# Expert stage of a graph layer: two row fetches and two result scatters in flight, alternating semaphores, four result buffers

## The chip, the core and the metric

The kernel runs on one core of one Trainium2 chip. The metric is the device time of one execution in microseconds (us). Five engines take part: PE multiplies matrices (PEld is its loading of weights), DVE is the vector engine, ACT the scalar engine, POOL the engine that also issues the indirect DMAs, SP a sequencer that issues plain DMAs. Engines are kept in order with semaphores alone.

## The reference, cut to what matters

A graph convolution gives 12500 rows of 256 numbers; each row is then sent to the two best of 64 experts, a small two-layer network each, and their results are weighted and added:

```python
logits = x @ Wg + bg
vals, idx = jax.lax.top_k(logits, 2)
gates = jax.nn.softmax(vals, axis=-1)
# per expert e, at most 1024 rows (CAP):
h1 = gelu(buf[e] @ w1[e] + b1[e])      # 256 -> 512, float32
h2 = h1 @ w2[e] + b2[e]                # 512 -> 256, float32
core = zeros.at[tok].add(gate * h2)    # each row gets two results
```

After it come a batch norm, a residual and a layer norm over all rows.

## The kernel before

The kernel has three long stages, one after the other. The first sorts out the edges and the degrees. The second, `aggregate`, gathers edge rows, sums them on PE, and routes each row to its experts; it ends at about 2412 us. The third is `experts`, from about 2416 to 3455 us, and then `norms` closes the kernel. Only `experts` (line 1460) is touched.

In `experts` the work is cut into turns. A turn is 128 rows of one expert. An expert has from one to a few turns, and the 64 experts have 228 turns in all with these inputs. Four experts' weights are held at a time (`HELD`), 1152 KB each.

What a turn n needs, engine by engine:

- POOL fetches its 128 rows out of `x1_rows` in HBM into slot n % 4 of `ring`, by an indirect DMA (`fetch`, line 1565). The indices are in `rows_at`.
- ACT copies the slot to `xs` (`take`, line 1543). PE transposes `xs` (line 1674), DVE copies the result to `xst` (line 1621).
- PE multiplies with w1 in four pieces (line 1681), ACT applies the Gelu to each piece (line 1548, `hid`), PE multiplies `hid` with w2 (line 1688).
- DVE adds the bias (line 1648, `ysum`), and in `scale` (lines 1629 to 1639) writes the indices of a later fetch into `rows_at`, the places of the results into `places`, works out the gates, and writes the scaled result to `ys`. It counts this in `y_set`.
- POOL scatters `ys` to `picked` in HBM by an indirect DMA (`send`, line 1573), with semaphore `y_sent[n % 2]`.

The order on each engine is written by hand. ACT does the four Gelus of turn n, then `take(n + 2)`; after the last turn of an expert it issues three DMAs for the weights of the expert three further on (`load_weights`, lines 275 to 277), and goes on to the next turn's Gelus. PE does w1 of turn n, the transpose for turn n + 1, then w2 of turn n. POOL does, for each turn n (`quad`, lines 1586 to 1595), one after the other:

1. wait until the scatter of turn n - 1 has landed, and count `freed`, which lets DVE write `places` and `ys` again (two buffers each);
2. wait for `y_set` of turn n, and issue the scatter of turn n;
3. wait until the fetch of turn n + 3 has landed (`rows_in`, one semaphore for all fetches), and issue the fetch of turn n + 4 into the slot that turn n has left.

So one fetch and one scatter are in flight at a time. ACT's `take` waits on the same semaphore `rows_in` directly. DVE rounds the number of turns up to a whole number of fours, so `scale`, scatter and fetch run for four more turns (228 to 231) after the last real one; these scatters point out of bounds and write nothing.

`bounds` loads, once for every four experts and on each engine, where their turns begin.

Of the kernel before, what the change touches and what calls it, by code (L numbers as in the profile page):

```python
# [18 lines left out]
F32 = mybir.dt.float32  # L19
BF16 = mybir.dt.bfloat16  # L20
I32 = mybir.dt.int32
# [4 lines left out]
P = 128  # L26
# [1433 lines left out]
def experts(nc, x1_rows, picked, w1s, w2s, b2s, w_in, load_weights, ident, table, base_of, b1_cols, ps, D, X, H, KD, KH, ROW, PLACES):  # L1460

    with ExitStack() as part:
        def t2(name, shape, dt):
            return part.enter_context(nc.sbuf_tensor(name, shape, dt))

        def sem2(name):
            return nc.alloc_semaphore(name)

        U = HELD
        R = 4  # L1470
# [3 lines left out]
        rows_at = t2("rows_at", [P, R], I32)  # L1474
        in_order = t2("in_order", [P, 4, X * SLOTS + 4 * SLOTS], F32)
        xs = t2("xs", [P, D], F32)
        xst = t2("xst", [P, KD, SUP], F32)
        places = t2("places", [P, 2], I32)
        second = t2("second", [P, 2], F32)
        gate = t2("gate", [P, 2], F32)  # L1480
        hid = t2("hid", [P, KH, SUP], F32)
        ysum = t2("ysum", [P, D], F32)
        ys = t2("ys", [P, 2, D], F32)
        warm = t2("warm", [P, 1], F32)

        rows_in = sem2("ring_in")
        first_rows_at = sem2("first_rows_at")
        order_set = sem2("order_set")
        xs_set = sem2("xs_set")
# [9 lines left out]
        y_sent = [sem2("y_sent0"), sem2("y_sent1")]  # L1499
        freed = sem2("ys_freed")  # L1500
        carrier = sem2("x_carrier")
# [8 lines left out]
        def turns_in_all(engine):  # L1510
            return nc.values_load(base_of[0:1, X:X + 1], engines=[engine], min_val=X, max_val=X * CAP // SUP,
                                  skip_runtime_bounds_check_because="the sum of the experts' turns")
# [21 lines left out]
        with nc.Block() as block:  # L1534
            @block.scalar
            def _(act):
                def take(g):

                    act.wait_ge(rows_in, 16 * (g + 1))

                    if not isinstance(g, int) or g > 0:
                        act.wait_ge(xs_turned, g)
                    nc.scalar.copy(xs[:, :], ring[:, g % R, 0:D]).then_inc(xs_set, 1)  # L1543

                def turn(e, u, g, g0):
                    for h in range(KH):
                        act.wait_ge(h_done, g * KH + h + 1)
                        nc.scalar.activation(hid[:, h, :], ps[:, h, 0:SUP], ACT.Gelu,  # L1548
                                             bias=b1_cols[:, h, bass.ds(e, 1)]).then_inc(h_set, 1)
                    take(g + 2)  # L1550

                def follow(e, u, g0):

                    act.wait_ge(ysum_set, g0 + 1)
                    load_weights(act, e, u)

                nc.scalar.activation(warm[:, :], b1_cols[:, 0, 0:1], ACT.Gelu)
                take(0)
                take(1)
                each_expert(act, EngineType.Activation, lambda *a: None, turn, follow)  # L1560

            @block.gpsimd
            def _(pool):
                def fetch(u):
                    pool.indirect_dma_start(out=ring[:, u, :], out_offset=None, in_=x1_rows[:, :],  # L1565
                                            in_offset=bass.IndirectOffsetOnAxis(ap=rows_at[:, u:u + 1], axis=0)).then_inc(rows_in, 16)

                def send(n, u):
                    b = u % 2
                    pool.wait_ge(y_set, n + 2)  # L1570
                    pool.sem_inc(carrier, 1)

                    pool.indirect_dma_start(out=picked[:, :], out_offset=bass.IndirectOffsetOnAxis(ap=places[:, b:b + 1], axis=0),  # L1573
                                            in_=ys[:, b, :], in_offset=None, bounds_check=PLACES - 1,
                                            oob_is_err=False).then_inc(y_sent[b], 16)

                pool.wait_ge(first_rows_at, 1)
                for u in range(R):
                    if u > 0:
                        pool.wait_ge(rows_in, 16 * u)  # L1580
                    fetch(u)
                pool.sem_inc(freed, 1)

                quads = (turns_in_all(EngineType.Pool) + R) // R

                def quad(j):
                    for u in range(R):
                        n = R * j + u
                        if not isinstance(n, int) or n > 0:
                            pool.wait_ge(y_sent[1 - u % 2], 32 * j + 16 * ((u + 1) // 2))  # L1590
                        pool.sem_inc(freed, 1)
                        send(n, u)
                        pool.wait_ge(rows_in, 16 * (n + R))
                        pool.sem_inc(carrier, 1)
                        fetch(u)
                quad(0)
                with pool.Fori(1, quads) as j:
                    quad(j)
                pool.wait_ge(y_sent[0], 32 * quads)
                pool.sem_inc(carrier, 1)  # L1600
                pool.wait_ge(y_sent[1], 32 * quads)
                pool.sem_inc(carrier, 1)
                pool.wait_ge(rows_in, 64 * quads + 64)
                pool.sem_inc(carrier, 1)

            @block.vector
            def _(dve):
                def put_in_order(e, at):

                    nc.vector.tensor_copy(in_order[:, :, bass.ds(at, SLOTS)], table[:, :, bass.ds(e * SLOTS, SLOTS)]).then_inc(order_set, 1)  # L1610

                starts = bounds(EngineType.DVE, 0)
                for e in range(U):
                    put_in_order(e, starts[e])
                    dve.wait_ge(order_set, e + 1)
                nc.vector.tensor_copy(rows_at[:, :], in_order[:, 0, 0:R]).then_inc(first_rows_at, 1)
                nc.vector.memset(ysum[:, :], 0.0).then_inc(ysum_set, 1)
                dve.sem_inc(y_set, 1)

                def keep_turned():  # L1620
                    nc.vector.tensor_copy(xst[:, :, :], ps[:, 6, 0:KD * SUP].rearrange("p (k n) -> p k n", k=KD)).then_inc(xst_set, 1)  # L1621
                dve.wait_ge(xs_turned, 1)
                keep_turned()

                def scale(n):


                    b = n % 2
                    nc.vector.tensor_copy(rows_at[:, bass.ds(n % R, 1)], in_order[:, 0, bass.ds(n + R, 1)])
                    nc.vector.tensor_scalar(second[:, 0:1], ring[:, n % R, D + 1:D + 2], in_order[:, 2, bass.ds(n, 1)], None,  # L1630
                                            ALU.mult).then_inc(gate_part_set, 1)
                    dve.wait_ge(freed, n + 1)
                    nc.vector.tensor_copy(places[:, bass.ds(b, 1)], in_order[:, 1, bass.ds(n, 1)])
                    dve.wait_ge(gate_part_set, n + 1)
                    nc.vector.scalar_tensor_tensor(gate[:, 0:1], ring[:, n % R, D:D + 1], in_order[:, 3, bass.ds(n, 1)], second[:, 0:1],
                                                   ALU.mult, ALU.add).then_inc(gate_set, 1)
                    dve.wait_ge(gate_set, n + 1)
                    dve.wait_ge(ysum_set, n + 2)
                    nc.vector.tensor_scalar(ys[:, bass.ds(b, 1), :].rearrange("p a d -> p (a d)"), ysum[:, :],
                                            gate[:, 0:1], None, ALU.mult).then_inc(y_set, 1)  # L1640

                def turn(e, u, g, g0):

                    dve.wait_ge(xs_turned, g + 2)
                    keep_turned()
                    dve.wait_ge(y_set, g + 1)
                    dve.wait_ge(y_done, g + 1)
                    nc.vector.tensor_tensor(ysum[:, :], ps[:, 4, 0:D], b2s[:, u, :], ALU.add).then_inc(ysum_set, 1)  # L1648
                    scale(g)

                def before(e, i, u, starts):

                    put_in_order(e + U, starts[U + u])
                    dve.wait_ge(order_set, e + U + 1)
                    dve.wait_ge(w_in[u], 48 * (i + 1))
                    dve.sem_inc(carrier, 1)
                each_expert(dve, EngineType.DVE, before, turn, more=U - 1)
                last = turns_in_all(EngineType.DVE)
                dve.wait_ge(xs_set, last + 2)
                dve.sem_inc(carrier, 1)  # L1660
                with dve.Fori(last, (last + R) // R * R) as n:
                    dve.sem_inc(ysum_set, 1)
                    scale(n)

            @block.tensor
# [305 lines left out]
```

## Time and profile before

| | us |
|---|---|
| median of 3 runs | 3764.92 |
| lowest and highest | 3763.87, 3767.51 |
| the profiled execution, its own time | 3769.93 |
| its span, first to last instruction | 3768.2 |
| PE busy in the span | 3028.5 (80%) |
| POOL busy | 2136.5 (57%) |
| DVE busy | 1867.6 (50%) |
| ACT busy | 1083.0 (29%) |

The span is that of the profiled execution, 1.7 us under its own time. The chain of work that ended last names little more than the end of the kernel, so the stage of interest has to be read from the time line and the waits. In the time line each line is: start in us, duration in us, engine, line of the kernel, operation, what it writes and reads, how many were merged, and in brackets the idle time of the engine just before and what ended it.

### The profile page before, as it was taken

Reading aid. Unit: us, or ns where it says so; the run is one execution under the profiler, and the core shown is the slowest. Engines: PE = TensorE matmul, PEld = TensorE weight load, DVE = VectorE, ACT = ScalarE, POOL = GpSimd, SP = SyncE. Lnnn points to the kernel's source line nnn. Section 1 sums busy time; section 2 is a strip of 40 time slices with the busy share of each in tenths; the row PEclk is TensorE's granted clock in tenths of the full one; section 3 lists DMA queues with packets and bytes.
Section 4 is the critical chain, followed back from the end, with each engine's and each line's share of the span. In section 5 each row is a group of like instructions: output and inputs, shape, how many; then the busy total and the mean of one; then the engine's idle time right before and its main releaser. Section 6 shows DMA issues by size and latency. Waiting matters only on the chain. (4 is left out here: it accounts for less than half of the span.)

```text
span 3768.2 us, 61533 instructions
## 1 busy us (share of the span) xinstructions
PE 3028.5 (80%) x16520; PEld 2198.4 (58%) x16684; DVE 1867.6 (50%) x6028; ACT 1083.0 (29%) x2679; POOL 2136.5 (57%) x2194
## 2 busy tenths in 40 slices
PE   3747889898899888898998898789888898894710
PEld 3523555555555555555555555588777887884610
DVE  6982444444444444444444444544443444443878
ACT  3950222222222222222222222233333333331123
POOL 3006777777777777777777777244444444442122
PEclk9878999999999999999999999899999999997865
DMA  8635444444444444444444444334344343434634
GB/s 351 223 102 159 126 118 128 128 118 128 128 117 128 118 128 128 117 129 127 118 128 121 125 117 118 112 120 133 120 134 147 118 131 124 136 121 135 204 107 145
DMA packets 287579, 509.98 MB, mean 135 GB/s; under 512 B 43417, under 2 KB 201200, under 8 KB 284738
## 3 DMA queue, kind: packets, MB, share of 16 engines
q0 software_dynamic: 102192, 274.64, 25.7%
q10 hardware_dynamic: 73042, 123.41, 9.4%
q1 hardware_dynamic: 112192, 109.95, 9.1%
q8 instruction: 89, 1.46, 0.2%
q14 instruction: 64, 0.52, 0.0%
HBM read 404.99 MB, written 107.63 MB: 136 GB/s over the span
## 5 line engine op out<-in xcount | busy, mean ns | idle before, releaser
L1150 POOL DMA_INDIRECT work<-h_table,src_cols x1661 | 1575.5, 949 | 728.0 <-issue 426.2
L1436 PE MATMUL ps<-work 128*128 128x257 f32 x3322 | 1063.2, 402 | 208.5 <-DMA work<-h_table,src_cols 185.2
L1436 PEld LDWEIGHTS ps<-work 128*128 128x128 f32 x3322 | 563.8, 192 | 556.5 <-issue 301.5
L1342 PE MATMUL ps<-none_w,none 128*128 128x512 bf16 x2213 | 677.1, 383 | 5.5 <-issue 0.4
L1565 POOL DMA_INDIRECT ring<-x_rows,rows_at x236 | 230.8, 978 | 484.8 <-DMA ring<-x_rows,rows_at 235.5
L1688 PE MATMUL ps<-work,hid 128*128 128x256 f32 x1824 | 445.0, 387 | 72.5 <-ACT hid L1548 70.5
L1681 PEld LDWEIGHTS ps<-xst,work 128*128 128x128 f32 x3648 | 444.9, 193 | 25.6 <-issue 13.4
L1681 PE MATMUL ps<-xst,work 128*128 128x128 f32 x3648 | 448.6, 276 | 8.2 <-issue 7.4
L1185 DVE TENSOR_TENSOR acc<-acc,ps 128x257 f32<-128x257 f32 x98 | 41.5, 423 | 780.6 <-PE ps L1333 780.6
L1688 PEld LDWEIGHTS ps<-work,hid 128*128 128x128 f32 x1824 | 328.7, 190 | 134.3 <-ACT hid L1548 97.9
L1342 PEld LDWEIGHTS ps<-none_w,none 128*128 128x128 bf16 x2344 | 224.7, 99 | 160.1 <-issue 3.8
L1548 ACT ACTIVATE hid<-ps,b_cols 128x128 f32<-128x128 f32 x912 | 269.2, 368 | 142.8 <-PE ps L1681 99.2
L1573 POOL DMA_INDIRECT picked<-ys,places x232 | 234.6, 1011 | 127.6 <-issue 100.9
L1648 DVE TENSOR_TENSOR ysum<-ps,work 128x256 f32<-128x256 f32 x228 | 96.9, 425 | 397.9 <-PE ps L1688 397.9
L1170 DVE TENSOR_TENSOR work<-rel_cols,ps 128x1152 f32<-128x1152 f32 x196 | 250.6, 1280 | 64.2 <-PE ps L1436 63.4
L1543 ACT COPY xs<-ring 128x256 f32 (+1 forms) x230 | 93.1, 405 | 509.6 <-DMA ring<-x_rows,rows_at 509.6
L1116 ACT COPY acc<-ps 128x256 f32<-128x256 f32 x98 | 36.6, 373 | 651.0 <-PE ps L1375 651.0
L1122 ACT COPY turned<-ps 128x512 f32<-128x512 f32 x98 | 57.4, 586 | 473.3 <-PE ps L1362 473.3
L733 ACT ACTIVATE stairs<-iota_f,lo_half 128x128 bf16<-128x128 f32 x624 | 183.0, 388 | 32.9 <-DVE lo_half L675 32.0
L1795 POOL TENSOR_TENSOR pk<-pk,beta_b 128x1792 f32<-128x1792 f32 x14 | 64.1, 4585 | 225.2 <-DMA pk<-in_x_dram 225.2
L1205 DVE TENSOR_TENSOR logits<-ps,gate_bias 128x64 f32<-128x64 f32 x98 | 22.0, 225 | 281.3 <-PE ps L1389 281.3
L1621 DVE COPY xst<-ps 128x256 f32<-128x256 f32 x229 | 97.3, 425 | 121.9 <-PE ps L1674 112.4
(256 smaller groups left out, 3806.4 us busy)
## 6 DMA issues: line engine op xcount, KB each, us to landing
work<-in_L_gnn_w_dram ACTq DMA_DIRECT2D x122, 512.0 KB, 4.6
work<-h_table,src_cols POOLq DMA_INDIRECT x1661, 2.8
picked<-acc ACTq DMA_DIRECT2D x1, 25088.0 KB, 102.1
pk<-picked SPq DMA_DIRECT2D x28, 896.0 KB, 8.1
m_base<-acc ACTq DMA_DIRECT2D x1, 12642.0 KB, 37.0
acc<-m_base SPq DMA_DIRECT2D x14, 903.0 KB, 6.5
x_rows<-acc SPq DMA_DIRECT2D x98, 129.0 KB, 2.4
xr_x<-in_x_dram SPq DMA_DIRECT2D x97, 128.0 KB, 2.3
```

What stands on the lines that cost most here:

```text
L733: mm = nc.scalar.activation(stairs[:, k, n, :], iota_f[:, :], ACT.Sign, scale=-1.0, bias=lo_half[:, bass.ds(g * PIECES + 2 * WHOLE + n, 1)])
L1150: pool.indirect_dma_start(out=got[:, c % RING, 0:D], out_offset=None, in_=h_table[:, :], in_offset=bass.IndirectOffsetOnAxis(ap=src_cols[: ...
L1170: nc.vector.tensor_tensor(hot[:, (2 * t + h) % HOTS, 0:b - a, :], rel_cols[:, a:b].unsqueeze(2).broadcast_to([P, b - a, P]), lanes.unsquee ...
L1342: nc.tensor.matmul(ps[:, 7, :], none[:, :], none_w[:, :], start=False, stop=False)
L1436: nc.tensor.matmul(ps_flat[:, bank(t, k, w[0])], hot[:, (2 * t + (k >= HALF)) % HOTS, k % HALF if k >= HALF else k, :], got[:, c % RING, : ...
L1548: nc.scalar.activation(hid[:, h, :], ps[:, h, 0:SUP], ACT.Gelu, bias=b1_cols[:, h, bass.ds(e, 1)]).then_inc(h_set, 1)
L1565: pool.indirect_dma_start(out=ring[:, u, :], out_offset=None, in_=x1_rows[:, :], in_offset=bass.IndirectOffsetOnAxis(ap=rows_at[:, u:u + 1 ...
L1573: pool.indirect_dma_start(out=picked[:, :], out_offset=bass.IndirectOffsetOnAxis(ap=places[:, b:b + 1], axis=0), in_=ys[:, b, :], in_offse ...
L1621: nc.vector.tensor_copy(xst[:, :, :], ps[:, 6, 0:KD * SUP].rearrange("p (k n) -> p k n", k=KD)).then_inc(xst_set, 1)
L1648: nc.vector.tensor_tensor(ysum[:, :], ps[:, 4, 0:D], b2s[:, u, :], ALU.add).then_inc(ysum_set, 1)
L1681: mm = nc.tensor.matmul(ps[:, h, 0:SUP], w1s[:, u, k, h * P:(h + 1) * P], xst[:, k, :], start=(k == 0), stop=(k == KD - 1))
L1688: mm = nc.tensor.matmul(ps[:, 4, 0:D], hid[:, h, :], w2s[:, u, h, :], start=(h == 0), stop=(h == KH - 1))
```

## The change

`rows_in` becomes two semaphores, used by turn for even and odd fetches. POOL issues the fetch of turn n + 4 right behind the scatter of turn n, without a wait between them. The wait for rows moves to the top of POOL's turn and is for the fetch of turn n + 2; behind it POOL counts a new semaphore `rows_ready`, and ACT's `take` waits for that in place of `rows_in`. The wait for a landed scatter is for turn n - 2 in place of n - 1. `places` and `ys` have four buffers in place of two. At the start two fetches are issued together. For the turns beyond the last, DVE waits for `rows_ready` too.

```diff
-        places = t2("places", [P, 2], I32)
+        places = t2("places", [P, R], I32)
-        ys = t2("ys", [P, 2, D], F32)
+        ys = t2("ys", [P, R, D], F32)
-        rows_in = sem2("ring_in")
+        rows_in = [sem2("ring_in0"), sem2("ring_in1")]
+        rows_ready = sem2("rows_ready")
...
-                    act.wait_ge(rows_in, 16 * (g + 1))
-
+                    act.wait_ge(rows_ready, g + 1)
...
-                                            in_offset=bass.IndirectOffsetOnAxis(ap=rows_at[:, u:u + 1], axis=0)).then_inc(rows_in, 16)
+                                            in_offset=bass.IndirectOffsetOnAxis(ap=rows_at[:, u:u + 1], axis=0)).then_inc(rows_in[u % 2], 16)
...
                 pool.wait_ge(first_rows_at, 1)
-                for u in range(R):
-                    if u > 0:
-                        pool.wait_ge(rows_in, 16 * u)
-                    fetch(u)
-                pool.sem_inc(freed, 1)
+                fetch(0)
+                fetch(1)
+                for u in range(2):
+                    pool.wait_ge(rows_in[u], 16)
+                    pool.sem_inc(rows_ready, 1)
+                    fetch(u + 2)
+                pool.sem_inc(freed, 2)
...
                 def quad(j):
                     for u in range(R):
                         n = R * j + u
-                        if not isinstance(n, int) or n > 0:
-                            pool.wait_ge(y_sent[1 - u % 2], 32 * j + 16 * ((u + 1) // 2))
+                        pool.wait_ge(rows_in[u % 2], 32 * j + 16 * (u // 2 + 2))
+                        pool.sem_inc(rows_ready, 1)
+                        if not isinstance(n, int) or n > 1:
+                            pool.wait_ge(y_sent[u % 2], 32 * j + 16 * (u // 2))
                         pool.sem_inc(freed, 1)
                         send(n, u)
-                        pool.wait_ge(rows_in, 16 * (n + R))
-                        pool.sem_inc(carrier, 1)
                         fetch(u)
...
-                    b = n % 2
+                    b = n % R
...
                 with dve.Fori(last, (last + R) // R * R) as n:
                     dve.sem_inc(ysum_set, 1)
+                    dve.wait_ge(rows_ready, n + 1)
+                    dve.sem_inc(carrier, 1)
                     scale(n)
```

## Rows read from the trace of the kernel before

**Rows 1.** Windows: length, busy PE, PEld, DVE, ACT, POOL, clock, DMA share, GB/s
```profile
2427.00:3427.00 1000.00, 894.91 (x5901) 805.18 (x5899) 426.81 (x1653) 358.53 (x1134) 450.74 (x453) 1.00 0.40 127
2613.31:2631.97 18.66, 18.66 (x132) 17.63 (x132) 9.50 (x36) 9.58 (x26) 9.94 (x10) 1.00 0.23 71
```

**Rows 2.** Groups from 2430 to 3420 us, and two lines: duration, first and last start
```profile
L1688 PE MATMUL ps<-work,hid 128*128 128x256 f32 x1795 | 437.7, 387 | 72.5 <-ACT hid L1548 70.5
L1543 ACT COPY xs<-ring 128x256 f32 x224 | 90.6, 405 | 496.9 <-DMA ring<-x_rows,rows_at 496.9
L1648 DVE TENSOR_TENSOR ysum<-ps,work x228: 424/425/426, 2427.0 to 3427.0; 128x256 f32<-128x256 f32 x114
L275 ACTq DMA_DIRECT2D work<-in_L_gnn_w_dram x61: 383/385/434, 2434.3 to 3393.5; - x61
```

**Rows 3.** Time line, two turns in which no transfer was late
```profile
2472.66 0.42 DVE L1648 TENSOR_TENSOR ysum<-ps,work 128x256 f32<-128x256 f32 x1 [1.37 <-PE ps L1688]
...
2473.89 0.35 DVE L1639 TENSOR_SCALAR ys<-ysum,gate 128x256 f32 x1 [0.15 <-DVE gate L1635]
...
2474.29 1.60 PEld L1688 LDWEIGHTS ps<-work,hid 128*128 128x128 f32 x8
...
2475.17 1.01 POOL L1573 DMA_INDIRECT picked<-ys,places  x1 [1.44 <-DVE ys L1639]
...
2476.09 0.39 ACTq L275 DMA_DIRECT2D work<-in_L_gnn_w_dram  x1
2476.40 0.42 DVE L1648 TENSOR_TENSOR ysum<-ps,work 128x256 f32<-128x256 f32 x1 [1.38 <-PE ps L1688]
2476.48 0.98 POOL L1565 DMA_INDIRECT ring<-x_rows,rows_at  x1 [0.30 <-issue]
...
2478.90 1.01 POOL L1573 DMA_INDIRECT picked<-ys,places  x1 [1.44 <-DVE ys L1639]
```

**Rows 4.** Time line, a change of expert, turns 53 to 55
```profile
2657.82 0.43 DVE L1648 TENSOR_TENSOR ysum<-ps,work 128x256 f32<-128x256 f32 x1 [1.37 <-PE ps L1688]
...
2658.26 0.40 ACT L1543 COPY xs<-ring 128x256 f32 x1 [1.96 <-DMA ring<-x_rows,rows_at]
...
2658.61 0.38 ACTq L275 DMA_DIRECT2D work<-in_L_gnn_w_dram  x1
...
2658.83 0.98 POOL L1565 DMA_INDIRECT ring<-x_rows,rows_at  x1 [1.24 <-DMA ring<-x_rows,rows_at]
...
2660.45 1.15 ACT L1548 ACTIVATE hid<-ps,b_cols 128x128 f32<-128x128 f32 x4 [1.78 <-PE ps L1681]
2660.86 1.59 PEld L1688 LDWEIGHTS ps<-work,hid 128*128 128x128 f32 x8 [1.39 <-ACT hid L1548]
...
2662.97 0.42 DVE L1648 TENSOR_TENSOR ysum<-ps,work 128x256 f32<-128x256 f32 x1 [2.67 <-PE ps L1688]
...
2664.57 0.40 ACT L1543 COPY xs<-ring 128x256 f32 x1 [2.98 <-DMA ring<-x_rows,rows_at]
...
2667.72 0.42 DVE L1648 TENSOR_TENSOR ysum<-ps,work 128x256 f32<-128x256 f32 x1 [1.79 <-PE ps L1688]
```

**Rows 5.** Time line, fetches one behind the other
```profile
2709.57 0.98 POOL L1565 DMA_INDIRECT ring<-x_rows,rows_at  x1 [1.26 <-DMA ring<-x_rows,rows_at]
...
2712.57 0.40 ACT L1543 COPY xs<-ring 128x256 f32 x1 [1.98 <-DMA ring<-x_rows,rows_at]
...
2713.14 0.98 POOL L1565 DMA_INDIRECT ring<-x_rows,rows_at  x1 [1.22 <-DMA ring<-x_rows,rows_at]
```

**Rows 6.** Windows at the change of expert, columns as in Rows 1
```profile
2659.00:2659.50 0.50, 0.50 (x7) 0.47 (x5) 0.46 (x2) 0.00 (x0) 0.50 (x1) 1.00 0.00 0
2661.50:2662.00 0.50, 0.50 (x4) 0.45 (x3) 0.00 (x0) 0.09 (x1) 0.00 (x0) 1.00 1.02 379
```

**Rows 7.** Time line, the end of the stage
```profile
3443.28 0.98 POOL L1565 DMA_INDIRECT ring<-x_rows,rows_at  x1 [2.42 <-DMA picked<-ys,places]
3443.31 0.15 DVE L1633 CAST places<-in_order  x1 [2.87 <-POOLq L1591]
...
3452.05 0.97 POOL L1565 DMA_INDIRECT ring<-x_rows,rows_at  x1 [2.10 <-DMA ring<-x_rows,rows_at]
```

More of the change, by code:

```diff
@@ L1565, in fetch @@
                     pool.indirect_dma_start(out=ring[:, u, :], out_offset=None, in_=x1_rows[:, :],
-                                            in_offset=bass.IndirectOffsetOnAxis(ap=rows_at[:, u:u + 1], axis=0)).then_inc(rows_in, 16)
+                                            in_offset=bass.IndirectOffsetOnAxis(ap=rows_at[:, u:u + 1], axis=0)).then_inc(rows_in[u % 2], 16)
                 def send(n, u):
-                    b = u % 2
                     pool.wait_ge(y_set, n + 2)
                     pool.sem_inc(carrier, 1)
-                    pool.indirect_dma_start(out=picked[:, :], out_offset=bass.IndirectOffsetOnAxis(ap=places[:, b:b + 1], axis=0),
-                                            in_=ys[:, b, :], in_offset=None, bounds_check=PLACES - 1,
-                                            oob_is_err=False).then_inc(y_sent[b], 16)
+                    pool.indirect_dma_start(out=picked[:, :], out_offset=bass.IndirectOffsetOnAxis(ap=places[:, u:u + 1], axis=0),
+                                            in_=ys[:, u, :], in_offset=None, bounds_check=PLACES - 1,
+                                            oob_is_err=False).then_inc(y_sent[u % 2], 16)
                 pool.wait_ge(first_rows_at, 1)
-                for u in range(R):
-                    if u > 0:
-                        pool.wait_ge(rows_in, 16 * u)
-                    fetch(u)
-                pool.sem_inc(freed, 1)
+                fetch(0)
[5 more added lines that the diff above has]
+                pool.sem_inc(freed, 2)
                 quads = (turns_in_all(EngineType.Pool) + R) // R
@@ L1602, in _ @@
                 pool.sem_inc(carrier, 1)
-                pool.wait_ge(rows_in, 64 * quads + 64)
-                pool.sem_inc(carrier, 1)
+                for u in range(2):
+                    pool.wait_ge(rows_in[u], 32 * quads + 32)
+                    pool.sem_inc(carrier, 1)
             @block.vector
```

## The prediction

> **What bounds the kernel now.** The chain of work that ended last covers only the last stage, so I began with windows over the expert stage. From 2427 to 3427 us PE is busy for 895 of 1000 us at full clock; in a quiet stretch of five turns, 2613.31 to 2631.97, it is busy all the time [rows 1]. So PE is the bound of a turn, at 3.73 us (18.66 / 5), and some 100 us of the stage is PE waiting. The groups say for what: before the w2 matmuls PE waits 72.5 us in all, 70.5 of it for ACT's Gelu, and ACT waits 497 us for fetched rows before `take` [rows 2].
>
> The size of the loss comes from the starts of line 1648, one for each turn; I call the start for turn n Y(n). The first of 228 is at 2427.0 (2426.96), the last at 3427.0 [rows 2]: 1000.0 us for 227 intervals, against 227 x 3.73 = 846.7. The excess is 153 us, and it is all that a better order of DMAs can win between these starts. Taking the differences of all the starts: 101 intervals are at 3.7 to 3.8. In 61 intervals ACT issues weights (line 275) [rows 2]; 43 of these are about 5.1 long (58 us of excess) and 18 about 6.0 (40 us; most of these are where the bounds of four experts are loaded). Of the intervals just behind them 47 are long, by 0.93 on average (44 us). The remaining ones hold 11 us.
>
> A change of expert shows the two mechanisms [rows 4].
> - First interval, 5.15 us: ACT takes rows at 2658.26, which is 0.44 behind Y (0.50 on average over the 61), issues three weight DMAs from 2658.61, and starts the Gelus at 2660.45, 2.19 behind the take. PE loads the first `hid` 0.41 later, at 2660.86. In a quiet turn this load is 1.63 behind Y (2474.29 less 2472.66) [rows 3]. So the excess of such an interval is (take - Y) + 2.60 - 1.63 = (take - Y) + 0.97, here 1.41: the take's lateness goes over one for one.
> - Second interval, 4.75 us: the fetch issued at 2658.83, 0.22 behind the weights, lands only at 2664.57, 5.74 behind its start; in a quiet turn the time is 3.00 [rows 5]. The take is 1.60 behind Y. Without weights to issue, a take may be up to 0.79 behind Y (1.63 less 0.42 for the copy and 0.42 for the first Gelu); what is over is lost.
>
> Why is the take late at all? With one fetch in flight each fetch costs 3.00 to land and 0.57 to the next start, 3.57 us a turn [rows 5]. PE's turn is 3.73. A delayed fetch is made good by 0.16 us a turn, and a delay comes every 228 / 64 = 3.6 turns. The fetches run behind for the whole stage, and ACT waits for each landing.
>
> **The change, part by part.**
>
> *Fetch not waiting for the one before.* In a quiet turn the result is written at 2474.24, 1.58 behind Y (2473.89 + 0.35), the scatter starts at 2475.17, Y + 2.51, the fetch at 2476.48, Y + 3.82, with only the 0.30 gap between them [rows 3]. After the change this is where each fetch should start: F(n+4) = Y(n) + 3.82. It lands at Y(n) + 6.8. POOL's work is 2.6 us a turn, under PE's 3.73, so POOL does not become the bound.
>
> *The rows counted by POOL.* This adds a wait in front of ACT. `rows_ready` for turn n + 2 is counted at the top of POOL's turn n, hence behind the fetch issued in turn n - 1, which starts at Y(n-1) + 3.82 = Y(n) + 0.09. Rows may have landed long before; the take can't start before that. How soon behind the start of a fetch does POOL's queue go on? In the tail a DVE instruction released by POOL's `freed`, which stands behind a fetch in the program, starts 0.03 us behind that fetch's start, while its 0.98 us have hardly begun [rows 7]. I allow 0 to 0.3, and take 0.15: the take is at Y + 0.25. That is under 0.79, so ordinary turns are not delayed. For the 61 intervals with weights it is 0.25 earlier than now (0.50): 61 x 0.25 = 15 us won. The other 83 us of them stay, as three issues by ACT ahead of the Gelus are not touched.
>
> *The second interval.* The take being at Y + 0.25, weights go out at Y + 0.60, and the fetch in flight started at Y + 0.09: 0.5 us ahead of the weights rather than 0.22 behind. The trace has no fetch there. The bounds: a scatter started 0.92 ahead of the weights (2475.17 to 2476.09) had landed in time for the next to start at 2478.90 with DVE's result as the last thing it waited for, so it took no longer than about 3 us [rows 3]; a fetch 0.22 behind takes 5.74 [rows 4]. A line between them gives some 4 us at 0.5 ahead. Next Y is 3.73 + 1.22 = 4.95 behind this one, and the take may be 0.79 later, at Y + 5.74; landing at Y + 0.09 + 4.0, or even + 5.4, with 0.15 for POOL's hop, is in time. Of the 44 us I take 36 as won; the bounds are 0 (landing at the end of the weights, however early the fetch) and 44.
>
> The Trainium skill, DMA: Bandwidth & Descriptors, Queues, rings and completion order, says that each DMA engine takes packets in turn from the queues that have work. By that rule a small fetch should pass the weights almost at once; the trace disagrees (5.74 against 3.00), and if the rule held for the earlier start the whole 44 us would go. The same page, Issuing engines are not separate DMA queues, says that all DMAs share the same 16 engines and interleave; by that rule two in flight would each be slower. In the 0.5 us from 2659.0, with a fetch underway, the engines moved nothing, and with weights 379 GB/s [rows 6]: a lone fetch is delay, not bandwidth, so two overlap except beside weights.
>
> *Later fetches behind a delayed one.* These are no longer held back, so the 11 us of other long turns shrink; but about every 55 turns POOL pauses by some 2.7 us ahead of a scatter, and with rows counted by POOL such a pause now reaches ACT at once, at up to 2 us each, four times. I set +3 and -5 (bounds +8, -8).
>
> *Scatter waiting for n - 2, four buffers.* DVE's writes were never what ended last in the body. Nothing there. In the tail it matters: from Y of the last turn (3427.0) to the last fetch (3452.05) are 25 us for the last scatter and four padding turns, one landing behind another [rows 7], about 4.7 each. With two in flight a padding turn costs half of a landing of some 4.2 plus the way through POOL, (4.2 + 0.7 + 1.3) / 2 = 3.1: 3.8 + 4 x 3.1 = 16.2. Won: 9 us (bounds 4 and 12; 12 is POOL's own 2.6 a turn). DVE's new wait there is for a count that POOL makes two turns ahead.
>
> *Nothing:* n % 4 for n % 2 in addresses, a few semaphore counts on POOL ahead of `y_set`, hidden by its wait for DVE (if that cover went, 0.1 x 228 = 20 us at worst, but POOL has a slack of 1.1 a turn); the start, where the first take is at most 0.1 later and the second some 1 us earlier under a PE that is busy with w1.
>
> **Sum.** 15 + 36 + 3 - 5 + 9 = 58 us. Against the profiled execution's own 3769.9 that gives 3711.9. The median of the runs is 5.0 lower, 3764.9, which gives 3707. A difference of 0.2%, 7.5 us, is about what a measurement tells from none.
>
> **Rivals.**
> - *Landing is tied to the weights' end (3745).* At 0.22 behind, the fetch landed 5.96 behind the first weights issue, which is where their traffic ends. If the same holds at 0.5 ahead, the second interval keeps its loss: the Gelus, weights and landing all shift together, and the hop adds 0.1 x 61 = 6. Then 15 - 6 + 3 - 5 + 9 = 16, with bounds to 28: some 3745. For it: 5.4 to 6.1 for all of these fetches, as if behind a backlog. Against it: the scatter 0.92 ahead.
> - *POOL's count comes too late (3813, slower).* If the count is made only when the fetch's 0.98 us on POOL are over, the take is at Y(n-1) + 3.82 + 0.98 + 0.15 = Y(n-1) + 4.95, and the limit of 0.79 makes every ordinary turn 4.16 instead of 3.73: 0.43 x 166 = 71 lost; with weights 0.3 x 61 = 18 lost; won are 36 and 9, less 5 in pauses. Net +49: 3813. It decides from the point where the count is over 0.55 later than I assume. Against it stand the 0.03 us of the tail [rows 7]; for it, that this is at a padding turn, where the scatter ahead was long done.
> - *Two in flight land no sooner (3757).* The fetches share one queue and the second lands a full 3 us behind the first. Then the chain stays at 3.5 a turn, and only part of the tail is won, some 4 to 8 us: 3757 to 3761. Against it: fetch and scatter already overlap, 1.31 apart, each within about 3 us [rows 3].
>
> **How the numbers follow.** Forecast 0.52, weights' end 0.24, late count 0.14, no overlap 0.10. The forecast's own range is from about 3680 (takes at Y, all of 44, no pauses felt, tail 12: 30 + 44 + 3 + 12 = 89, 3676, not all at once) to 3730; with the second rival the range is 3680 to 3752, leaving out the third and part of the fourth. Faster by over 0.2% (under 3757): 0.52 + 0.24 + 0.03 = 0.79. Within: 0.08. Slower: 0.13.
>
> **What would show it.** Right: PE busy in the stage at some 94% of the time in place of 89%; starts of line 1648 at 3.73 in all turns but those with weights; take 0.2 to 0.3 behind Y everywhere, released by POOL; fetch starts at Y + 3.82; intervals with weights still near 4.9 and 5.8; last fetch 16 us behind the last Y. Wrong: intervals behind the weights still at 4.6 (first rival), ordinary turns above 4 (second), takes still 3.5 apart and a fetch's landing at 5 or more in quiet turns (third).

## The result

The changed kernel takes 3676.35 us (median of 4 runs, 3674.57 to 3676.73), the kernel before 3765.05 beside it. The ratio is 0.9763, with a 95% interval of 0.9746 to 0.9780: 89 us less, where 58 were forecast, and 4 us under the low end of the range. The direction was right and the mechanism half right; the size was wrong.

Windows of the changed kernel over the stage, then over its tail (columns as in [rows 1]):

```profile
2424.30:3343.10 918.80, 882.10 (x5902) 802.43 (x5900) 409.69 (x1652) 385.64 (x1134) 449.67 (x453) 1.00 0.44 139
3343.10:3360.00 16.90, 0.00 (x0) 0.00 (x0) 5.63 (x26) 0.40 (x1) 10.32 (x11) 0.63 0.26 48
```

PE is now busy for 96% of the time between the first and the last Y (882.1 / 918.8), against 89% before [rows 1]. Groups of the changed kernel from 2427 to 3340 us, to set beside [rows 2]; line 1548 is the Gelu, 1572 the scatter, 1565 the fetch:

```profile
L1692 PE MATMUL ps<-work,hid 128*128 128x256 f32 x1805 | 436.9, 385 | 12.4 <-ACT hid L1548 10.1
L1572 POOL DMA_INDIRECT picked<-ys,places x226 | 228.2, 1010 | 396.6 <-DVE ys L1641 372.5 <-issue 24.1
L1565 POOL DMA_INDIRECT ring<-x_rows,rows_at x226 | 220.4, 975 | 76.1 <-issue 74.3 <-DMA ring<-x_rows,rows_at 1.8
L1543 ACT COPY xs<-ring 128x256 f32 x226 | 91.6, 405 | 298.4 <-POOLq L1591 298.4
```

PE's wait before the w2 matmuls fell from 72.5 to 12.4 us (the part for `hid` from 70.5 to 10.1). In front of the fetch the program now has no wait for landed rows; that wait is ahead of the scatter, and most of the 24.1 us there that the profile puts down to "issue" are 11 gaps of about 2 us in turns whose rows landed late. ACT's take waits for POOL's queue (line 1591, the count of `rows_ready`), and these 298 us of waiting cost little, as they mostly fall where ACT has nothing else to do.

Where the 93 us between the two spans (3768.2 and 3675.0) went, by the starts of line 1648, now 1650:

| | before | after | difference |
|---|---|---|---|
| first Y to last Y, 227 intervals | 1000.0 | 918.8 | -81.2 |
| last Y to the start of the last fetch | 25.1 | 16.5 | -8.6 |
| up to the first Y | 2427.0 | 2424.3 | -2.7 |
| behind the last fetch | 316.2 | 315.4 | -0.8 |

The first Y is anywhere from 2422 to 2430 us in the kernels below (but for one run on a chip with a lower clock), so the third line of the table is no effect that I can claim.

For the intervals I use one more split below, worked out from all starts of the takes and of `ysum`: an interval with a *late take* is one whose take starts over 0.79 us behind Y, the limit from the prediction; the excess is over 3.73 us.

| | late takes | their excess | excess of the others |
|---|---|---|---|
| before | 68 | 62 | 91 |
| after | 45 | 37 | 35 |

The others' excess is nearly all in intervals in which ACT issues weights, or that begin four experts.

A quiet turn after the change:

```profile
2679.21 0.42 DVE L1650 TENSOR_TENSOR ysum<-ps,work 128x256 f32<-128x256 f32 x1 [1.58 <-PE ps L1692]
...
2680.43 0.35 DVE L1641 TENSOR_SCALAR ys<-ysum,gate 128x256 f32 x1 [0.16 <-DVE gate L1637]
...
2681.70 1.01 POOL L1572 DMA_INDIRECT picked<-ys,places  x1 [2.20 <-DVE ys L1641]
...
2682.57 0.40 ACT L1543 COPY xs<-ring 128x256 f32 x1 [1.18 <-POOLq L1591]
...
2682.94 0.42 DVE L1650 TENSOR_TENSOR ysum<-ps,work 128x256 f32<-128x256 f32 x1 [1.37 <-PE ps L1692]
...
2683.02 0.98 POOL L1565 DMA_INDIRECT ring<-x_rows,rows_at  x1 [0.30 <-issue]
```

and the instruction that counts the rows in it (a source line, from 2681.43 to 2683.2 us):

```profile
L1591 POOLq EVENT_SEMAPHORE  x1: 17/17/17, 2682.3 to 2682.3; - x1
```

Scatter and fetch start at Y + 2.49 and Y + 3.81, as forecast. But the count is made at 2682.3, 0.6 behind the scatter's start and 0.7 *ahead* of the fetch's, though it stands behind the fetch in the program. In other turns in which no rows are late it comes mostly 0.3 to 0.8 behind the scatter's start. The take is 0.37 ahead of the next Y, not 0.25 behind it.

The same change of expert as in [rows 4], after:

```profile
2636.88 0.41 ACT L1543 COPY xs<-ring 128x256 f32 x1 [0.83 <-POOLq L1591]
...
2637.24 0.38 ACTq L275 DMA_DIRECT2D work<-in_L_gnn_w_dram  x1
2637.61 0.42 DVE L1650 TENSOR_TENSOR ysum<-ps,work 128x256 f32<-128x256 f32 x1 [1.37 <-PE ps L1692]
2637.68 0.97 POOL L1565 DMA_INDIRECT ring<-x_rows,rows_at  x1 [0.30 <-issue]
...
2639.08 1.15 ACT L1548 ACTIVATE hid<-ps,b_cols 128x128 f32<-128x128 f32 x4 [1.79 <-PE ps L1685]
2639.49 1.59 PEld L1692 LDWEIGHTS ps<-work,hid 128*128 128x128 f32 x8 [0.23 <-ACT hid L1548]
...
2641.60 0.42 DVE L1650 TENSOR_TENSOR ysum<-ps,work 128x256 f32<-128x256 f32 x1 [1.52 <-PE ps L1692]
...
2643.17 0.40 ACT L1543 COPY xs<-ring 128x256 f32 x1 [2.95 <-POOLq L1591]
...
2646.32 0.42 DVE L1650 TENSOR_TENSOR ysum<-ps,work 128x256 f32<-128x256 f32 x1 [1.79 <-PE ps L1692]
```

The first interval went from 5.15 to 3.99 us: the take is 0.73 ahead of Y, the weights go out ahead of Y too, and the Gelus start 1.47 behind it, not 2.63. The second is 4.72 against 4.75, unchanged: the fetch is again behind the weights' first issue, by 0.44 where it was 0.22, and its rows are taken 5.49 us behind its start.

### The profile page after: what moved, and what is told of

Same layout as the page of the kernel before. It is cut to its first block and busy times, and to the rows that moved or that the text cites. A ratio compares the mean times of both kernels' runs of the same rounds, so it can differ in the third digit from the quotient of the medians.

```text
span 3675.0 us, 61427 instructions
## 1 busy us (share of the span) xinstructions
PE 3017.3 (82%) x16520; PEld 2188.2 (60%) x16684; DVE 1851.0 (50%) x6028; ACT 1110.4 (30%) x2679; POOL 2131.3 (58%) x2194
## 5 line engine op out<-in xcount | busy, mean ns | idle before, releaser
L1692 PE MATMUL ps<-work,hid 128*128 128x256 f32 x1824 | 441.6, 385 | 12.4 <-ACT hid L1548 10.1
L1548 ACT ACTIVATE hid<-ps,b_cols 128x128 f32<-128x128 f32 x912 | 297.7, 368 | 237.6 <-PE ps L1685 206.4
L1799 POOL TENSOR_TENSOR pk<-pk,beta_b 128x1792 f32<-128x1792 f32 x14 | 63.2, 4516 | 225.4 <-DMA pk<-in_x_dram 225.4
```

Source lines behind the costliest of these rows:

```text
L1692: mm = nc.tensor.matmul(ps[:, 4, 0:D], hid[:, h, :], w2s[:, u, h, :], start=(h == 0), stop=(h == KH - 1))
```

## The experiments

The theory (A): the gain is the take that comes early enough for ACT to issue the weights ahead of the Gelus' time, which needs two fetches in flight; late landings beside the weights' traffic are a second loss, only partly helped. The rival (B): the gain is in the scatters, for which POOL no longer waits.

In all these kernels the numbers of turns that the engines load are masked once more (`& 1023`), which the control measures. I compare the *stage*, from the first Y to the start of the last fetch, in the profiled execution: 1025.1 us before, 935.3 after. It comes from one execution of each kernel; the one kernel that was profiled twice on chips of like clock gave 898.4 and 899.9. The whole times scatter more, since the last stage of the kernel (`norms`), which nothing here touches, has two modes, 28 us apart (see the last section); the stage doesn't contain it.

### The control

```diff
-            return g
+            return tuple(nc.s_assert_within(x & 1023, 0, X * CAP // SUP, ...) for x in g)
```

> The changed kernel with one thing more: the numbers of turns that each engine loads for four experts are masked with 1023 (a register operation or two for each value, some 16 times an engine), which all the kernels below have too. Control for the others. If that costs nothing: 3676 us, as the changed kernel. If the register operations lie on PE's path: 16 x 0.2 us, 3680 us at most.

Measured: 3683.7 us (3649.8 to 3688.8), ratio 0.9776 (0.9760 to 0.9793); the stage is 940.7 us. So the mask costs some 5 us by the stage, a little over what was allowed (by the whole times it can't be told from nothing, as the ratio's interval overlaps that of the changed kernel), and 940.7 is what the next ones are held against. Late takes: 39 with 32 us; others 45 us.

### Scatters as before, fetches as after

```diff
-        places = t2("places", [P, R], I32)
+        places = t2("places", [P, 2], I32)
-        ys = t2("ys", [P, R, D], F32)
+        ys = t2("ys", [P, 2, D], F32)
...
-                        if not isinstance(n, int) or n > 1:
-                            pool.wait_ge(y_sent[u % 2], 32 * j + 16 * (u // 2))
+                        if not isinstance(n, int) or n > 0:
+                            pool.wait_ge(y_sent[1 - u % 2], 32 * j + 16 * ((u + 1) // 2))
...
```

> Scatters one in flight with two buffers, as before the change; fetches two in flight and rows counted by POOL, as after. Theory A (the gain is the early take: POOL's queue counts the rows some 0.7 us ahead of its fetch's start, ACT takes them ahead of Y, and the weights go out before the Gelus are due): the body keeps most of its gain, and what is lost is the tail (5 padding landings one behind another, +5 us) and turns in which weights delay a scatter that POOL then waits for (0 to 40 us): 3682 to 3720. Theory B (the gain is in the scatters, as POOL no longer waits for the one before): back to 3745 or more.

Measured: 3694.6 us (3688.0 to 3696.0), ratio 0.9798 (0.9782 to 0.9814); stage 947.8, 7 over the control, of which 1 is in the tail, where 5 were expected. Rival B is out.

### Fetches as before, scatters as after

```diff
-                        if not isinstance(n, int) or n > 0:
-                            pool.wait_ge(y_sent[1 - u % 2], 32 * j + 16 * ((u + 1) // 2))
+                        if not isinstance(n, int) or n > 1:
+                            pool.wait_ge(y_sent[u % 2], 32 * j + 16 * (u // 2))
```

and four buffers, on the kernel before.

> Fetches one in flight on one semaphore, and ACT waiting for their landing itself, as before the change; scatters two in flight with four buffers, as after. Theory A: the chain of fetches stays at 3.57 us a turn against PE's 3.73, takes stay behind Y, excess over 3.73 a turn stays near 150 us, and the tail is no shorter, since each padding turn still waits for a landed fetch: 3755 to 3765 us. Theory B: most of the gain, 3690 us or less.

Measured: 3760.2 us (3754.0 to 3764.5), ratio 0.9970 (0.9958 to 0.9981); stage 1014.4, body 989, tail 25.3. The tail is as long as before, the body 11 us shorter. Two fetches in flight, with the rows counted by POOL, carry the change; the scatters' part is small by itself: 11 us without the fetches (16 if the mask's 5 are taken off), 7 with them.

### The weights' traffic taken away

```diff
-                eng.dma_start(w1s[:, u, :, :], w1[bass.ds(e, 1), :, :].rearrange(...)).then_inc(w_in[u], 16)
+                eng.dma_start(w1s[:, u, :, 0:hh], w1[bass.ds(e, 1), :, 0:hh].rearrange(...)).then_inc(w_in[u], 16)
```

with `hh` a sixteenth of H, and the same for w2 and b2, in the 61 loads by ACT. This kernel leaves out most of each expert's weights and computes with what is left of older ones; it serves the timing alone.

> The changed kernel with the 61 weight loads that ACT issues cut to a sixteenth of their columns, so the three issues by ACT stay and the traffic goes (the experts then use weights that are mostly left over: part of the computation is left out). If late landings come from the weights' traffic: no fetch takes over 3.5 us, the 37 us of excess in turns whose take is over 0.79 behind Y go, the 35 us in turns with the three issues stay: 3640 us. If a fetch is late because of the issues themselves (queue or descriptors) and not the bytes: landings stay at 5.5 us and the time at 3676.

Measured: 3649.2 us (3635.1 and 3663.3), stage 917.9, 23 under the control. Late takes fall from 39 to 4, their excess from 32 to 5 us; the others keep theirs (50 against 45). So late landings are the bytes of the weights, not their issue. The four that are left are 55 turns apart, at turns 55, 110, 165 and 220 (counted from 0), each interval 4.96 to 5.02 us. The first of them:

```profile
2643.09 0.98 POOL L1566 DMA_INDIRECT ring<-x_rows,rows_at  x1 [0.30 <-issue]
...
2646.02 1.01 POOL L1573 DMA_INDIRECT picked<-ys,places  x1 [1.96 <-DVE ys L1642]
...
2647.23 0.42 DVE L1651 TENSOR_TENSOR ysum<-ps,work 128x256 f32<-128x256 f32 x1 [1.37 <-PE ps L1693]
...
2649.14 0.98 POOL L1566 DMA_INDIRECT ring<-x_rows,rows_at  x1 [2.11 <-issue]
2649.19 0.41 ACT L1544 COPY xs<-ring 128x256 f32 x1 [3.51 <-POOLq L1592]
```

POOL stops for 2.11 us between scatter and fetch, and the take, 1.96 behind Y, waits for it. That is the pause I had priced at 5 us in all: 4 x 1.25 = 5.

### The count made late

```diff
                         pool.wait_ge(rows_in[u % 2], 32 * j + 16 * (u // 2 + 2))
-                        pool.sem_inc(rows_ready, 1)
...
                         send(n, u)
+                        pool.sem_inc(rows_ready, 1)
                         fetch(u)
```

> The changed kernel with POOL's count of ready rows moved from the top of its turn to behind the scatter's issue, which waits for DVE's result (Y + 1.6). Does a late take cost PE one for one beyond 0.79 behind Y? If so (theory A), with the count at Y + 1.7 to Y + 2.5 the take is 1.0 to 1.8 too late in every turn, every interval is 4.7 to 5.5 us, and the time 3900 to 4080 us. If late takes are mostly absorbed (the gain is then elsewhere): under 3750 us.

Measured: 4173.3 us (one run). An ordinary turn:

```profile
2787.11 0.42 DVE L1651 TENSOR_TENSOR ysum<-ps,work 128x256 f32<-128x256 f32 x1 [1.64 <-PE ps L1693]
...
2789.61 1.01 POOL L1573 DMA_INDIRECT picked<-ys,places  x1 [3.23 <-DVE ys L1642]
2789.63 0.40 ACT L1544 COPY xs<-ring 128x256 f32 x1 [3.90 <-POOLq L1596]
...
2792.64 0.43 DVE L1651 TENSOR_TENSOR ysum<-ps,work 128x256 f32<-128x256 f32 x1 [1.64 <-PE ps L1693]
```

The take is 2.52 behind Y and the turn 5.53 long: 1.80 over 3.73. One for one from a limit of 2.52 - 1.80 = 0.72, near the 0.79 of the prediction. That it is one for one, the smaller delays show: in the control, lateness less excess is 0.73 in the middle of the 39 late takes (0.72 to 0.81), for takes 0.8 to 2.2 behind Y. The time is above the expected span, as the 61 intervals with weights came to 8.6 us each, which I had not counted. This is the slower rival's mechanism at full strength: a count in the wrong place costs 490 us against the control. It also says where the queue goes on here: behind a scatter in front of which POOL was free, about when the scatter starts.

### Weights issued by SP, on the kernel after

```diff
+            @block.sync
+            def _(sp):
+                def four(i, n):
+                    starts = bounds(EngineType.SP, U * i)
+                    for u in range(n):
+                        sp.wait_ge(ysum_set, starts[u] + 1)
+                        load_weights(sp, U * i + u + U - 1, (u - 1) % U)
...
```

and no weights issued by ACT.

> The changed kernel with the 61 weight loads issued by SP, as soon as the slot is free (the expert before is done, at its last Y + 0.5), instead of by ACT between two turns. Theory A: ACT no longer has three issues ahead of the Gelus, so of the 45 us in turns whose take is in time only PE's own load of bounds stays (16 x 0.6 = 10): -30. The traffic now starts 0.4 to 0.5 us behind the start of the fetch in flight, the case of my prediction that the trace of before didn't have: if a fetch that far ahead lands in time, another -25; if not, 0. Stage 941 to 885 (ahead is enough) or 911 us (it isn't).

Measured: 3641.5 us (3614.9 to 3642.0), ratio 0.9644 (0.9607 to 0.9680); stage 898.4, 42 under the control, between the two expected. The others' excess is 15 us, from 45. The late takes are 41 still (39 in the control), but with 21 us in place of 32. One of them, turn 36:

```profile
2565.63 0.42 DVE L1657 TENSOR_TENSOR ysum<-ps,work 128x256 f32<-128x256 f32 x1 [1.37 <-PE ps L1699]
2565.72 0.97 POOL L1572 DMA_INDIRECT ring<-x_rows,rows_at  x1 [0.30 <-issue]
2566.23 0.37 SPq L275 DMA_DIRECT2D work<-in_L_gnn_w_dram  x1
...
2569.36 0.42 DVE L1657 TENSOR_TENSOR ysum<-ps,work 128x256 f32<-128x256 f32 x1 [0.95 <-PE ps L1699]
...
2570.27 0.40 ACT L1544 COPY xs<-ring 128x256 f32 x1 [2.46 <-POOLq L1598]
```

This is the case that the trace of before did not have: a fetch 0.51 ahead of the weights. It is taken 4.55 us behind its start, against 3.00 alone [rows 5] and 5.74 when 0.22 behind [rows 4]; over the 51 fetches 0.5 to 0.6 ahead in this run the middle value is 4.61 (4.3 to 6.0). The line that I drew between the bounds gave 4.0. The take is 0.91 behind Y, just over the limit.

### Weights issued by SP, on the kernel before

The same edit, nothing of the change.

> The kernel before with the weight loads issued by SP, nothing else of the change. If the loss before the change is mostly ACT's three issues behind a late take (theory A, 91 us in turns whose take is in time for an ordinary turn): they go without two fetches in flight, stage 1025 to some 945 us, and the late landings (62 us) stay or grow. If the fetch chain alone sets the pace: under 30 us won, 995 us or more.

Measured: 3755.1 us (3752.6 to 3758.9), ratio 0.9971 (0.9959 to 0.9984); stage 1015.7. Theory A as I had put it here was wrong: not 80 us, but 9. The others' excess did fall, from 91 to 16 us, but that of the late takes rose from 62 to 128. A change of expert:

```profile
2518.86 0.37 SPq L275 DMA_DIRECT2D work<-in_L_gnn_w_dram  x1
...
2519.46 0.98 POOL L1572 DMA_INDIRECT ring<-x_rows,rows_at  x1 [1.42 <-DMA ring<-x_rows,rows_at]
...
2521.98 0.42 DVE L1655 TENSOR_TENSOR ysum<-ps,work 128x256 f32<-128x256 f32 x1 [0.71 <-PE ps L1695]
2525.30 0.40 ACT L1544 COPY xs<-ring 128x256 f32 x1 [4.73 <-DMA ring<-x_rows,rows_at]
...
2528.30 0.42 DVE L1655 TENSOR_TENSOR ysum<-ps,work 128x256 f32<-128x256 f32 x1 [1.65 <-PE ps L1695]
```

The fetch starts 0.60 behind the weights here, as it had to wait for the one before. The first interval is 3.73 and the next 6.32. With one fetch in flight the fetches set the pace: time that ACT no longer loses is lost at the next landing. The same edit is worth 42 us with two fetches in flight and 9 with one (14 with the mask taken off).

### Fetch ahead of the scatter

```diff
-                        send(n, u)
-                        fetch(u)
+                        pool.wait_ge(y_set, n + 2)
+                        pool.sem_inc(carrier, 1)
+                        fetch(u)
+                        send(n, u)
```

> The changed kernel with the fetch of turn n + 4 issued ahead of the scatter of turn n, both behind DVE's result: the fetch starts at Y + 2.5 instead of Y + 3.8, the scatter 1.3 later. A fetch beside weights lands some 5.7 us behind its start, now 1.3 earlier against the take. If such landings hang on the fetch's start: the 32 us of late takes in the control fall to 10 or less, stage (first Y to start of last fetch) 941 to 918 us. If they hang on the end of the weights' traffic: they stay, 941 us.

Measured: 3654.0 us (3653.2 to 3655.2), ratio 0.9700 (0.9683 to 0.9716); stage 911.0, 30 under the control. Late takes fall to 9 with 7 us, and the tail by 3 us. The fetch starts at Y + 2.4, 1.1 or 1.5 ahead of the weights in most changes of expert. POOL's count moves too (the take in the turns without weights is 0.72 ahead of Y in the middle, 0.27 in the control), but that isn't the gain: the others' excess stays at 44 us against 45.

### Both

> The changed kernel with both: fetch ahead of the scatter, and weights issued by SP. With SP alone the stage (first Y to start of last fetch) was 898.4 us, with 20.7 us of excess in 41 turns whose take was late by some 0.9 us behind Y; with the fetch 1.3 us earlier those takes should be in time: 20 less, and some 3 less as the last fetch starts 1.3 earlier and pauses are met sooner: 875 to 880 us, and 23 us under the run with SP alone in the whole. If the two gains are the same one (a fetch no longer beside the weights' start): 898 us. If a scatter 1.3 us later, beside the weights, holds POOL: over 905 us.

Measured on a chip on which the kernel before takes 4116 us, with a mean granted clock of 0.887: 3974.4 us, ratio 0.9654 (0.9637 to 0.9672). The stage is 882.2 there. To have it beside SP alone on a chip like the others, both were run once more:

> The kernel with weights issued by SP once more, as the run with both edits fell on a chip with a lower clock, to have the two side by side: 3641 us and a stage of 898 us, if this chip's clock is that of the earlier runs.

> Both edits once more, on one chip with SP alone: by the late takes that are left with SP alone (20.7 us) the stage is 875 to 880 us and the time 20 to 25 us under SP alone. If the gains overlap: the same as SP alone.

Measured: SP alone 3642.4 us (3640.6 to 3645.5), ratio 0.9669 (0.9653 to 0.9686), stage 899.9. Both edits 3609.3 us (3594.4 to 3626.4), ratio 0.9570 (0.9531 to 0.9609), stage 880.7, where 875 to 880 were expected. The second edit is worth 19 us of the stage here and 30 alone, since SP alone had already taken 11 of the 32 us of late takes: together they won 60 us, not 42 + 30. (The median of 3609.3 lies between two runs near 3595 and two near 3625, the two modes of `norms`; the stage is free of that.) Of 227 x 3.73 = 847 us of PE, 21 us of excess are left: 7 in six late takes, four of them the pauses, and 14 mostly where four experts' bounds are loaded. It beats both kernels.

## Why the prediction was wrong

The excess over 3.73 us a turn in the prediction's own classes, and the tail, each worked out from all starts in the two traces:

| | before | after | won | forecast |
|---|---|---|---|---|
| the 61 intervals in which ACT issues weights | 99.2 | 35.1 | 64.1 | 15 |
| the 61 just behind them | 42.6 | 34.1 | 8.5 | 36 |
| all other intervals | 11.5 | 2.9 | 8.6 | -2 |
| tail | 25.1 | 16.5 | 8.6 | 9 |

The sum is 89.8 where 58 were forecast, and the first two terms were off by 49 and by 28 in opposite directions. That the time missed the range by only 4 us is luck: the low end's own sum, 30 + 44 + 3 + 12 = 89, is right with hardly a term in it right.

- **What bounds the kernel.** Right. PE's 3.73 us is the length of an undelayed turn in every kernel here but the one with the late count, where each turn is delayed; the excess fell from 153 to 72 us, and with both edits to 21.
- **Fetch at Y + 3.82, scatter at Y + 2.51.** Right: the medians are 3.81 and 2.49.
- **The rows counted by POOL.** The step that failed. I let the count come 0 to 0.3 us behind the *start* of the fetch ahead of it, and took that from one pair in the tail, 0.03 us apart [rows 7]. That pair was misread: the 3443.31 is the start of the DVE instruction that the count released, and the count itself stands in the same trace at 3443.08, 0.20 us *ahead* of the fetch's start, although it had to wait for a landed scatter there. In the body POOL's queue hands over an indirect DMA while POOL still works on the one before, and goes on: the count is mostly 0.5 to 1.1 us ahead of the fetch's start. I gave this unknown no bound on the early side. My formula, one for one, was right: the mean take in the 61 intervals with weights moved from 0.44 behind Y to 0.64 ahead of it (0.44, since my 0.50 was a mean with some takes misplaced), which makes 61 x 1.08 = 66 us. I had 15; measured are 64.
- **The second interval.** 36 forecast, 8.5 measured, and this term failed as a consequence. The premise was a fetch 0.5 us ahead of the weights, with 5.5 us or so to land in. Earlier takes pull ACT's weights forward too, so the fetch is behind them as before (0.3 us on average). They also pull the next Y forward, from 4.95 behind this one to 3.99 in the case above, so a landing tied to the weights has that much less time. The rival of the weights' end priced this term nearly rightly for this kernel, but its reason, a landing at the weights' end however early the fetch, doesn't hold: at 0.51 ahead the rows are taken after 4.55 us, and at 1.1 ahead they land in 2.8 (median), as if alone. The Trainium skill, DMA: Bandwidth & Descriptors, Queues, rings and completion order, says that each DMA engine takes packets in turn from the queues that have work. By that the fetch would pass the weights, if its packets were in their queue; no run shows it passing them. In the trace of the changed kernel, behind the fetch that started at 2637.68, not one packet of POOL's queue starts from 2638.5 to 2641.4, while ACT's queue moves the weights (2638.4 to 2642.6); in the quiet turn above the fetch's packets start some 1.5 us behind it. Whether the delayed packets stand in their queue all this time or are not there yet isn't shown.
- **Pauses and other turns.** Net -2 forecast, +8.6 measured. The price of a pause was right, by the run with small weights: 4 x 1.25. But the kernel before had paid for pauses as well (the interval behind the first one is 6.12 us, 2.39 over), which I had not set against it, and nothing but pauses is left over in the changed kernel's other intervals.
- **Tail.** 9 forecast, 8.6 measured, from 25.1 to 16.5 us, by the mechanism given.
- **Rivals.** The late count was out in this kernel and real as a mechanism, by the run with the count moved. No overlap of two fetches was out: fetches start every turn at Y + 3.81, and in the control they land in 2.8 us (median), as before the change. The price of the weights' end, "some 3745", doesn't follow from its own sum, which gives 3765 - 16 = 3749.

One kernel was not run: two fetches in flight with ACT waiting for the landings itself. How much of the gain hangs on the early count, and not on the second fetch alone, stays open.

## What to carry to other kernels

When a wait on one engine is replaced by a count that another makes in program order, find the time of the count itself in the trace, for instructions that stand in a like place, and not the start of what it released; look in the body and not in the tail, and bound it on both sides. A loss behind a wait may move and not go: taking ACT's issues away was worth 9 to 14 us with one fetch in flight and 42 with two, and two edits that go for the same late rows won 60 us together, not 72. So the order in which such edits are tried decides what each seems to be worth. Where a small transfer runs beside a large one, start it earlier: 1.3 us gave 30.

## What the runs showed of the hardware

- When two indirect DMAs are back to back, POOL's queue passes the second 0.6 us behind the start of the first (median; mostly 0.3 to 0.8), 0.7 ahead of its own start; when POOL is free it passes it at its start (take at Y + 2.52, scatter at Y + 2.50).
- How late a 129 KB fetch lands beside 1152 KB of weights depends on its start against the weights' first issue. From its start to its landing the medians are 2.8 us alone, 2.8 at 1.1 ahead (fetch first), 4.4 at 0.1 ahead (control), and 5.4 at 0.2 behind (before; 5.2 to 6.4). ACT takes the rows some 0.2 us later. With a sixteenth of the bytes and the same issues the delay is gone.
- Every 55 turns, that is every 110 indirect DMAs, POOL pauses: it is idle for 2.1 to 2.3 us in the kernels with two fetches in flight, and for 2.9 to 4.0 where the ordinary wait comes on top, at the same turns (within one) in all of them. What it does then no run shows.
- The stage behind, `norms`, took some 316 us in most profiled executions and 286 to 288 in three (the control, the late count and the small weights). The lines that differ, in the changed kernel and in the control:

```profile
L1842 DVE TENSOR_TENSOR acc<-acc,pk 128x1792 f32 (+1 forms) x14 | 72.0, 5145 | 0.6
```

```profile
L1843 DVE TENSOR_TENSOR acc<-acc,pk 128x1792 f32 (+1 forms) x14 | 39.3, 2809 | 0.6
```

  One DVE addition with both operands in SBUF takes 5145 or 2809 ns, while POOL adds to the same kind of tile with 4516 or 4916 ns each. The Trainium skill, SBUF — State Buffer, SBUF: two separate sides, says that such a DVE operation and a GpSimd operation that reads SBUF hold one pair of ports in turn, for a whole instruction each; that fits, and which of them comes first would be the mode. It was not tried. The difference between the modes, 28 us, is my estimate of what there is to gain in executions in the slower one.
